# Query projection ahead of the third scores, value products behind them, and a front of its own, in an attention and adapter kernel on one core

## What is computed

```python
q = rope(rmsnorm(x @ Wq.T) * q_norm_w)      # 32 heads
k = rope(rmsnorm(x @ Wk.T) * k_norm_w)      # 8 heads
v = x @ Wv.T                                # 8 heads
k_all = concat(k_cache[block_table], k)     # 512 cached + 128 new keys per batch
v_all = concat(v_cache[block_table], v)
scores = q @ k_all.T / sqrt(128)            # cached keys beyond cache_seqlens are masked
x = x + softmax(scores) @ v_all @ Wo.T
```

## Time and profile before

| what | value |
| --- | --- |
| runs (median; lowest, highest) | 1185.21 us (1185.18, 1185.74) |
| the profiled execution's own time | 1183.14 us |
| its span in the profile | 1181.3 us |
| TensorE matmuls (PE) | busy 1146.3 us, 97% |
| VectorE (DVE) | busy 923.3 us, 78% |
| ScalarE (ACT) | busy 932.1 us, 79% |
| GpSimd (POOL) | busy 766.3 us, 65% |
| chain that ended last | PE 87%, DVE 5%, ACT 3%, issue 2% |
| TensorE idle for the first turned queries (L1115) | 9.1 us, once |
| TensorE idle at turned probabilities (L1042) | 6.6 us |
| HBM traffic | 82 GB/s over the span |

### The profile page before, as it was taken

One profiled execution on the slowest core, in us unless ns is written; L12 is line 12 of the kernel. 1 busy time (PEld: TensorE's weight loads), 2 busy tenths in 40 slices (PEclk: granted clock), 3 DMA queues, 4 the chain that ended last, 5 costly groups with the idle time before them and its releaser, 6 DMA issues.

```text
span 1181.3 us, 20774 instructions
## 1 busy us (share of the span) xinstructions
PE 1146.3 (97%) x6912; PEld 1024.1 (87%) x6912; DVE 923.3 (78%) x1880; ACT 932.1 (79%) x1830; POOL 766.3 (65%) x838
## 2 busy tenths in 40 slices
PE   4799999999999999999999999999999999999898
PEld 3688898998899898989988998989899889989787
DVE  6788888787778777887877787778878777877746
ACT  3787888888888888888888888888888888888741
POOL 5566666677676667676766766677667667666500
PEclk9899999999999999999999999999999999999999
DMA  6423412221232222122212222221232122111001
GB/s 240 127 79 97 148 53 89 95 88 54 94 95 70 72 94 95 51 91 94 88 55 95 94 66 77 94 95 50 93 94 83 58 93 92 59 67 55 19 1 72
DMA packets 53626, 98.11 MB, mean 83 GB/s; under 512 B 8592, under 2 KB 25872, under 8 KB 53264
## 3 DMA queue, kind: packets, MB, share of 16 engines
q1 hardware_dynamic: 41232, 63.21, 15.4%
q0 software_dynamic: 12288, 33.57, 9.6%
HBM read 90.45 MB, written 6.29 MB: 82 GB/s over the span
## 4 chain that ended last, share of the span: by engine, by line
PE 87%; DVE 5%; ACT 3%; issue 2%; DMA 1%; SPq 1%; POOL 0%; DVEq 0%; POOLq 0%
PE ps_s L1011 18%; PE ps_w L282 17%; PE ps_w L280 17%; PE ps_w L281 17%; PE ps_w L1042 9%; PE ps_w L1133 3%; PE ps_w L1115 2%; PE ps_s L993 2%; PE ps_w L1019 2%; ACT ps L527 2%; DVE pt_lo L664 1%; ACT ps L533 1%; DMA y<-wo 1%; DVE ps L727 1%; PE ps_w L1032 1%
## 5 line engine op out<-in xcount | busy, mean ns | idle before, releaser
L406 POOL DMA_INDIRECT kv_raw<-kv,rows x256 | 253.6, 991 | 93.8 <-issue 62.7
L527 ACT ACTIVATE ps<-ps,negmax 128x640 f32<-128x640 f32 x256 | 211.9, 828 | 97.9 <-DVE negmax L727 97.8
L664 DVE TENSOR_TENSOR pt_lo<-ps_w,pt_hi 128x512 fp32r<-128x512 f32 x322 | 209.9, 683 | 75.7 <-ACT pt_hi L538 74.4
L533 ACT ACTIVATE ps<-ps,recip 128x640 f32<-128x640 f32 x256 | 213.0, 832 | 67.4 <-DVE recip L734 67.4
L727 DVE CUSTOM_DVE_ANT_0 ps<-ps_s,mask 128x640 f32<-128x640 f32 x256 | 203.8, 814 | 1.1 <-PE ps_s L1011 1.1
L280 PE MATMUL ps_w<-w_hi,xt_hi 128*128 128x512 f32 (+1 forms) x512 | 188.9, 369 | 10.0 <-DVE w_lo L664 8.3
L282 PE MATMUL ps_w<-w_hi,xt_lo 128*128 128x512 f32 (+1 forms) x512 | 173.6, 339 | 0.0
L281 PE MATMUL ps_w<-w_lo,xt_hi 128*128 128x512 f32 (+1 forms) x512 | 173.1, 338 | 0.0
L427 POOL TENSOR_TENSOR rot<-u,cos 128x640 f32<-128x640 f32 x64 | 101.5, 1587 | 110.0 <-DVE u L783 110.0
L538 ACT ACTIVATE pt_hi<-ps_w 128x512 fp32r<-128x512 f32 x256 | 151.7, 593 | 17.8 <-PE ps_w L1042 15.0
L1042 PE MATMUL ps_w<-cst,ps 128*128 128x128 f32 x1024 | 154.1, 273 | 6.6 <-DVE pt_lo L664 5.9
(11 more groups left out here) (155 smaller groups left out, 2625.0 us busy)
## 6 DMA issues: line engine op xcount, KB each, us to landing
xt_hi<-xsplit SPq DMA_DIRECT2D x56, 256.0 KB, 3.2
xt_lo<-xsplit SPq DMA_DIRECT2D x56, 256.0 KB, 3.7
w_raw<-wqkv SPq DMA_DIRECT2D x56, 192.0 KB, 3.9
wo_raw<-wo SPq DMA_DIRECT2D x56, 128.0 KB, 4.2
kv_raw<-kv,rows POOLq DMA_INDIRECT x256, 3.9
xsplit<-xt_hi SPq DMA_DIRECT2D x8, 256.0 KB, 2.9
xsplit<-xt_lo SPq DMA_DIRECT2D x8, 256.0 KB, 4.2
y<-x SPq DMA_DIRECT2D x2, 1024.0 KB, 7.4
```

The lines of the kernel that those rows point to most:

```text
L406: pool.indirect_dma_start(kv_raw[:, g % 2, t, :], None, kv[:, :], bass.IndirectOffsetOnAxis(rows[:, g % B, t:t + 1], 0)).then_inc(s_kv[g % ...
L527: nc.scalar.activation(ps[:, h, :], ps[:, h, :], ACT.Exp, bias=negmax[:, s % 2, h:h + 1], scale=-1.0, accum_out=rowsum[:, s % 2, h:h + 1]) ...
L533: nc.scalar.activation(ps[:, h, :], ps[:, h, :], ACT.Copy, scale=recip[:, s % 2, h:h + 1]).then_inc(a_norm, 1)
L664: return nc.vector.tensor_tensor(out_ap, full, hi.bitcast(F32), ALU.subtract)
```

## The change

It has four parts. (1) In a step, TensorE computes the queries of g2 right behind scores 0 and 1, then scores 2, then the values of s - 1; ScalarE and VectorE follow with their reads (on VectorE o_lo now comes behind the sine product m). `UNITS` starts with Q instead of O ahead of T0. (2) Steps -2 and -1 are replaced by a front written out by hand on each engine: key and value weights are loaded and split first, g = 0 is multiplied by the plain norm weights, rotated on VectorE and scaled by the inverse norms afterwards, in five pieces on two engines; TensorE starts with WARM = 20 transposes. The angle is reduced in two parts instead of three. (3) The splits of the first output weights, the masks of batches 2 to 7, the split of x tile 3 and the bias rows move into steps 0, 1, 2 and 8. (4) The tables of the weight pieces change, with a second place in a step (`W_MID`, `WO_MID`); x tiles 2 and 3 are split into space of the second weight buffer. Natural x comes in eight loads instead of two.

The core of the diff, with "..." where lines are left out:

```diff
-TWO_PI_A = 6.28125
-TWO_PI_B = float(np.float32(int((TWO_PI - TWO_PI_A) * 2**20) / 2**20))
-TWO_PI_C = float(np.float32(TWO_PI - TWO_PI_A - TWO_PI_B))
+TWO_PI_A = round(TWO_PI * 2**12) / 2**12
+TWO_PI_B = float(np.float32(TWO_PI - TWO_PI_A))
...
-UNITS = ["O", "T0", "Q", "T1", "Y", "T2", "QT", "KTC", "KV", "KTN", "T3", "TN"]
+UNITS = ["Q", "O", "T0", "T1", "Y", "T2", "QT", "KTC", "KV", "KTN", "T3", "TN"]
...
-W_AT = {}
-for h in range(1, HK + 1):
-    for j in range(B):
-        W_AT.setdefault((0, 0, 1, 2, 2, 3, 4, 4)[j] if h == 1 else B * h - 11 + j, []).append((h - 1) * B + j)
-WO_AT = {s: [s] for s in range((HK - 1) * B + 2)}
+W_AT = {2: [2], 3: [4], 4: [6], 5: [7]}
+W_MID = {1: 0, 2: 1, 3: 3, 4: 5}
+for n in range(B, HK * B):
+    W_AT[n - 2] = [n]
+WO_AT = {3: [0], 4: [1], 5: [2], 6: [4], 7: [6], 8: [7]}
+WO_MID = {6: 3, 7: 5}
+for n in range(B, (HK - 1) * B + 2):
+    WO_AT[n + 1] = [n]
 RING = 3
+WARM = 20
...
+        def split_cols(g):
+            if 2 <= g < HB:
+                return w_hi[:, 1, (g + 2) * KC * S:(g + 3) * KC * S], w_lo[:, 1, (g + 2) * KC * S:(g + 3) * KC * S]
+            return xt_hi[:, g % 2, :], xt_lo[:, g % 2, :]
...
             def natural_x(half):
 
                 sp.wait_ge(d_xlo, (half + 1) * HB)
-                sp.dma_start(y[:, half * HB:(half + 1) * HB, :], x[half * HB:(half + 1) * HB].rearrange("b s h -> s b h")
-                             ).then_inc(s_y[half], 16)
+                for j in range(HB):
+                    sp.dma_start(y[:, half * HB + j, :], x[half * HB + j]).then_inc(s_y[j], 16)
...
-            for s in range(-2, G):
+            for s in range(G):
+                if s == 0:
+                    keep_x(2)
+                    keep_x(3)
+                    natural_x(0)
+                    sp.wait_ge(d_wolo, REP)
+                    x_transposed(2, 1, 0, 4)
+                if s + 1 in W_MID:
+                    w_load(W_MID[s + 1])
                 for n in W_AT.get(s + 1, ()):
                     w_load(n)
...
+                elif n == B - 3:
+                    act.wait_ge(pe_kv, HB)
+                    act.wait_ge(s_xkept[0], 64)
+                    act.wait_ge(s_xkept[1], 64)
...
```

ScalarE, in a step (the reads of queries and exponential 2 now ahead of o_hi):

```diff
+                if has(g2):
+                    queries(g2)
+                turn_x(s, "Q")
+                if has(s):
+                    if HB <= s + 3 < B:
+                        split_x(s + 3)
+                    exps(2)
+                    norm(2)
                 if has(s - 1):
                     wait(act, pe_o, s - 1)
...
                 if has(s):
                     probs(1)
+                    if s in W_MID:
+                        w_split(W_MID[s])
+                    if s in WO_MID:
+                        wo_split(WO_MID[s])
                     exps(3)
...
```

VectorE, in a step and in the front:

```diff
+                if s in (1, 2):
+                    masks(3 * s - 1, 3 * s + 1)
                 for n in W_AT.get(s - 1, ()):
                     w_split(n)
                 for n in WO_AT.get(s - 1, ()):
                     wo_split(n)
+                if has(s):
+                    rowmax(2)
+                if s == 0:
+                    split_x(3)
+                if has(g1):
+                    wait(dve, p_wr, g1 - 1)
+                    wait(dve, d_ss, g1)
+                    nc.vector.tensor_tensor(u[:].rearrange("p h d -> p (h d)"), raw[:, g1 % 2, 0:QW + D],
+                                            wr[:].rearrange("p h d -> p (h d)"), ALU.mult).then_inc(d_u, 1)
+                if has(s):
+                    over_sum(2)
+                if has(g1):
+                    times_sine(g1)
                 if has(s - 1):
                     wait(dve, a_o, s - 1)
                     low(o_lo[:], bank("O"), o_hi[:]).then_inc(d_olo, 1)
...
+                if HB <= s + 3 < B:
+                    split_x(s + 3)
+                if s == 0:
+                    first_wo_split(0)
+                    first_wo_split(1)
                 if has(s):
                     probs(2)
...
+                if s in W_MID:
+                    w_split(W_MID[s])
+                if s in WO_MID:
+                    wo_split(WO_MID[s])
+                if has(g1):
+                    new_keys(g1)
+                if s in (1, 2):
+                    masks(3 * s + 1, 3 * s + 2)
...
+                if s == B:
+                    biases()
...
+            first_kv_low(1)
+            less_turns(TWO_PI_A)
+            first_w_low(0)
+            less_turns(TWO_PI_B)
+            for k in range(1, KC):
+                first_w_low(k)
...
+            nc.vector.tensor_tensor(u[:].rearrange("p h d -> p (h d)"), raw[:, 0, 0:QW + D], nw[:].rearrange("p h d -> p (h d)"),
+                                    ALU.mult).then_inc(d_u, 1)
+            sums_of_squares(0)
+            dve.wait_ge(d_tab, 1)
+            times_sine(0)
+            dve.wait_ge(a_sincos, 2)
+            nc.vector.tensor_tensor(rot[:].rearrange("p h (t d) -> p (h t) d", t=2), u[:].rearrange("p h (t d) -> p (h t) d", t=2),
+                                    cos[:, 0, :].unsqueeze(1).to_broadcast([P, 2 * NH, HALF]), ALU.mult).then_inc(d_cos, 1)
...
+            for h in range(2, NH):
+                nc.vector.tensor_scalar(rot[:, h, :], rot[:, h, :], rstd[:, h:h + 1], None, ALU.mult).then_inc(d_scaled, 1)
...
+            masks(0, 2)
+            for s in range(G + 1):
                 step(s)
```

TensorE:

```diff
+            def project_queries(g):
+                if g < B:
+                    pe.wait_ge(d_xlo, g + 1)
+                else:
+                    pe.wait_ge(s_xback[g % 2], 32 * ((g - B) // 2 + 1))
+                    if g % B == 0:
+                        pe.wait_ge(d_wlo, SPLITS + g)
+                if g >= 2:
+                    wait_bank(pe, g - 2, "Q")
...
                     scores(1)
                 if s == G:
                     second_layer(0)
+                if has(g2):
+                    project_queries(g2)
+                turn_x(s, "Q")
+                if has(s):
+                    scores(2)
                 if has(s - 1):
...
+                if s == 0:
+                    project_keys_values(g2)
...
+            pe.wait_ge(s_cst, 16)
+            for _ in range(WARM):
+                nc.tensor.transpose(ps_s[:, 0, 0, 0:P], ident, ident)
+            pe.wait_ge(d_xlo, 1)
+            project_keys_values(0)
+            project_queries(0)
+            project_queries(1)
+            turn_cached_keys(0)
+            project_keys_values(1)
+            turn_queries(0)
+            turn_new_keys(0)
+            for s in range(G + 1):
                 step(s)
```

More of the change, by code:

```diff
@@ L876, in _ @@
+            dve.wait_ge(d_rot, 2)
+            wait(dve, p_rstd, 0)
+            for h in range(2, NH):
+                nc.vector.tensor_scalar(rot[:, h, :], rot[:, h, :], rstd[:, h:h + 1], None, ALU.mult).then_inc(d_scaled, 1)
+            cached_keys(0)
+            split_x(2)
+            turned_queries(0)
+            new_keys(0)
+            dve.wait_ge(s_kpos, 16)
+            masks(0, 2)
+            for s in range(G + 1):
                 step(s)
@@ new lines, in turn_new_keys, with project_keys_values, between @@
+            def turn_new_keys(g):
+                if g == 0:
+                    wait(pe, a_kv, 0)
+                else:
+                    wait_bank(pe, g - 1, "KTN")
+                nc.tensor.transpose(bank("KTN")[:, 0:S], rot[:, REP, :], ident).then_inc(pe_ktn, 1)
+            def project_keys_values(g, new_keys_of=None):
+                if g == 1:
+                    wait(pe, a_q, 0)
+                elif g >= 2:
+                    wait_bank(pe, g - 2, "KV")
+                def between(k):
+                    if g == 0:
+                        pe.wait_ge(d_wlo, k // 2 + 1)
+                    if new_keys_of is not None and k == KC - 1:
+                        turn_new_keys(new_keys_of)
+                wh, wl = head_weights(g // B)
+                three_passes(keys_values_bank(g)[:, 0:2 * D], [(xt_tile(0, g, k), xt_tile(1, g, k), wh[:, k, QW:WW], wl[:, k, QW:WW])
+                                                      for k in range(KC)], before=between).then_inc(pe_kv, 1)
@@ new lines, in turn_queries, with turn_cached_keys @@
+            def turn_queries(g):
+                if g == 0:
+                    pe.wait_ge(a_scaled, 2)
+                    pe.wait_ge(d_scaled, NH - 2)
+                    wait(pe, a_q, 1)
+                else:
+                    wait(pe, p_rot, g - 1, 2)
+                    wait_bank(pe, g - 1, "QT")
+                for h in range(REP):
+                    last = nc.tensor.transpose(bank("QT")[:, h * S:(h + 1) * S], rot[:, h, :], ident)
+                last.then_inc(pe_qt, 1)
+            def turn_cached_keys(g):
+                wait_kv(pe, g)
+                wait_bank(pe, g - 1, "KTC")
+                for t in range(CT):
+                    last = nc.tensor.transpose(bank("KTC")[:, t * P:(t + 1) * P], kv_raw[:, g % 2, t, 0:D], ident)
```

(1 more changed line is left out.)

415 lines of the change are left out of this document (202 added, 213 removed).

## The result

| what | before | changed |
| --- | --- | --- |
| runs, us (median; lowest, highest) | 1185.20 (1185.18, 1185.74) | 1224.12 (1222.40, 1225.85) |
| ratio to before, 95% interval | 1 | 1.0327 [1.0309, 1.0345] |
| profiled execution, span | 1183.14, 1181.3 | 1224.33, 1222.5 |
| mean granted clock (share of full speed) | 0.994 | 0.976 |

The change makes the kernel 38.9 us slower. The forecast was 1211 us with a range of 1197 to 1226; the time lies between it and the range's top, 5 us above rival 1 (seven falls of the clock, 1219).

The account below looks back on a forecast made before the run. TensorE's own stream was taken to bound the kernel, 17.10 us a step. Terms summed to +26.3 on the profiled 1183.14 (1209.4), 1211.5 at the runs' median, given as 1211; range 1197 to 1226.

Parts of the forecast that it names:

- rival 1: All seven stalls of TensorE drop its clock to half: 7.5 us more, 1219 us; chance 0.25.
- Part 1, front: Work ahead of the first scores: shorter chain to them, 11 us won (bounds 8 and 14), first scores near 23.
- step 0: VectorE's queue sets this step, with output weight splits and masks at its head: 1 us off, between 0 and 4.
- steps 1 to 5: Added work moves to where VectorE idles, some overruns delay row maxima: 3 us off, between 0 and 5.
- bias rows, o_lo chain, other effects in steps 6 to 61: Bias rows delay step 9's first row maximum, 1.5 us once; o_lo just in time, 0.03 a step, 1.5 us.
- falls of the clock: Stalls may drop TensorE's clock, 2.1 us each: none to seven falls, 0 to 15, half taken, 7.5 us on.
- tail: Steps 62 and 63: without queries the output product comes early, meets o_lo and turned x: 1 us on, -1 to 3.
- term (a): In the front: without output weights in between, the square of the queries starts earlier; 5.5 less 1, 4.5 us won.
- rival 2: VectorE's sine product loses the race to GpSimd's: output product 0.8 late in some 55 steps, 44 more, 1255; chance 0.10.
- Part 4: Queries wait for a head's last weight piece, split in the same step: 4.26 us, seven times, 29.8 on.
- Rival 3: The last weight piece is ready in time, so the stalls cost nothing: faster, 1174 us; chance 0.07.
- Rival 4: Stalls are there, but early steps don't gain as splits push the row maxima: 1216 us; 0.58 jointly with forecast.

Follow-up runs that it names:

- Experiment 3: Changed kernel with weight pieces split a step earlier and the old order of a step on all engines, new front kept; chip A: 1176.57 us, ratio 0.9931.
- 11: The same kernel as Experiment 3 (old order, early weight table, new front), timed again on chip C: 1175.44 us, ratio 0.9916.
- Experiments 1: Kernel before with only the weight table changed, each piece split one step later; chip A: 1184.23 us, ratio 0.9992.
- experiment 9: Changed kernel with weight pieces split a step earlier, the same program as experiment 2, on chip C: 1179.41 us, ratio 0.9947.
- Experiment 6: Changed kernel with 36 unused transposes ahead of each of the seven waits for the last weight piece; chip B: 1248.71 us, ratio 1.0539.
- experiment 5: Changed kernel with early weight table, VectorE's turned x split ahead of o_lo, bias rows halved over steps 8 and 9; chip A: 1213.35 us, ratio 1.0247.
- experiment 2: Changed kernel with weight pieces split a step earlier; chip A: 1218.92 us, ratio 1.0289.
- experiment 10: The kernel of experiment 9 with a memset of an unused tile on VectorE ahead of the sine product; chip C: 1178.36 us, ratio 0.9941.
- experiment 4: Changed kernel, unchanged, timed again on chip B: 1264.73 us, ratio 1.0673 to the kernel before.

## Why the prediction was right, and where it was off

In the terms of the sum, in spans (1181.3 to 1222.5, +41.2; the forecast's sum was +26.3):

| step of the prediction | forecast | measured |
| --- | --- | --- |
| Part 1, front | -11 | -9.7 |
| step 0 | -1 | +0.9 |
| steps 1 to 5 | -3 | -2.1 |
| bias rows, o_lo chain, other effects in steps 6 to 61 | +3 | -1.5 |
| seven stalls (queries 4.26 later; measured 4.24) | +29.8 | +29.7 |
| falls of the clock | +7.5 | +17.5 |
| tail | +1 | +6.4 |

The number fell into the range by luck in part: the same program took 1264.73 us on chip B, 39 above the range, by a delay that no term or rival has.

**Front.** Right in mechanism, 1.3 off, and all of it in term (a). Against 4.5 + 5.1 + 1.8 and 0.4 off for the rest, the trace gives 3.1 + 5.2 + 1.8 and 0.4 off: the square starts at 16.85 and not near 15.4, m at 18.36, the last sum ends at 20.91, the first scores start at 24.26. The square waits for the queries, which ScalarE reads only at 16.19. In the other profiles with this front the first scores lie between 23.2 and 26.3, so 1.3 is within what differs from run to run. Experiment 3 shows that this part is the gain.

**Steps 0 to 5.** The forecast took 1 us off step 0 where 0.9 came on. With the old order and the same front step 0 takes 17.32 (experiments 3 and 11) and with the new order 18.03 to 18.07 in all profiles but one, so 0.7 of it belongs to the new order; the rest may be the splits and masks at its head. What the fall of the clock at 36.83 costs in it isn't shown.

**The order in a step.** The hand timeline held to 0.02 us at every point of an ordinary step, and with it the claim that o_lo arrives just in time. The bias rows cost 1.0 in step 9 (18.07) instead of 1.5. The ordinary step is 0.05 below 17.10 rather than 0.03 above it; that is the negative entry (steps 6 to 61 took 1003.5 instead of 957.8 us, +45.7, less 29.7 and 17.5). What I didn't see is how much hangs on "just in time". I had noted 0.1 us of margin and put a chance on one way of losing it, the race. On two of the chips it was lost by another, a late signal of the scores, for 40 us. "m at 0.82" was right for ordinary steps only: in the seven long ones the race was lost, by rival 2's own condition (row maximum 2 started at 12.45 of step 30, against "later than about 6.4"), and cost nothing.

**The stalls.** Part 4 is right in place, number and length: the queries start 6.08 into the step against 6.10, 4.24 later than the 1.84 of an ordinary step, seven times. (TensorE's idle time is shown as 4.1, since the product before ends at 2.00.) Experiments 1 and 9 show that both parts of the change are needed for them.

**The clock.** This is the step that was mis-sized. "From none to seven falls, I take half" should have been seven (rival 1, chance 0.25, is what happened), and each cost 2.5 us instead of 2.1: 47.2 over the ordinary step, less 29.7, over seven. Experiment 6 gave 2.4 by itself. The Trainium skill's rule on idle gaps between bursts (TensorE: Matmul & The Clock Gate, "Why this matters for your kernels") was the better guide here, and the trace agrees: every one of the seven pauses of 4.1 us lowered the clock. I had weighed it against an idle of 2.4 us that did no harm, which said nothing about 4, and not even about 2.4: in step 0 of the changed kernel the clock fell behind an idle of 2.42, with another of 0.44 and four transposes just ahead of it, and in step 62 during one of 3.53.

**The tail.** The forecast's 1 covered "the turned x" without following it. `turn_x` moved with the queries on every engine; on VectorE it ended behind the split of probabilities 0, and by the renamed banks the output product waits for it. Steps 62 and 63 needed a hand timeline of their own, as the ordinary step had. In experiment 5, where that split stands ahead, step 62 and what follows it are 6.9 us shorter than in experiment 2.

Rival 3 (ready in time) is out by the rows above. Rival 4 (no gain in early steps) lies nearer than the forecast: steps 0 to 5 gained 1.2 us together, where 4 were forecast and rival 4 has none. Rival 2's price in an ordinary step stays unmeasured after experiment 10.

**What stays open** is why the signals of scores 0 and 1 come late on chips A and B. The profile shows when they rise, not why. They are there with both tables and both orders, and experiment 9's program has them on A and not on C, so neither table nor order alone makes them. But the order bears on their size: on chip A the old order has 40 of some 250, by 0.9 us at most (experiments 1 and 3), the new one 110, by up to 1.7 (experiments 2 and 5). What they have in common is the place, the first 4 us of a step, where the loads for the next steps run. The kernel before was timed on all three within 1 us but profiled once, so that it meets them on A and B and absorbs them is inferred from experiments 1 (40 late signals, and 1184.23 us) and 3.

## What to carry to other kernels

When a consumer moves forward in an engine's order, look up every producer's place in the step for the worst instance (here the head's last piece), not for the usual one; and do it for the last steps, where other work takes the banks. A stall of TensorE like these has to be priced with its fall of the clock, here 4.2 us for the wait and 2.5 for the clock each, and shorter idles shouldn't be counted free on the strength of one that was. A dependency that is met within 0.1 us can't be relied on: move its producer ahead of work that nobody waits for (o_hi ahead of a normalisation), and time the kernel on more than one chip before believing it.

## What the runs showed of the hardware that was not expected

- Completion signals of TensorE's score products reached VectorE 0.2 to 1.7 us after the product's modelled end, in 110 of 251 cases in experiment 2 (chip A), in 111 of 251 in experiment 4 (chip B) and in none of the four profiles on chip C. All of them were due in the first 2 us of a step. The same program took 1218.92 and 1179.41 us.
- Transposes raised and held TensorE's clock: behind 20 of them at 3.23 us a product at 8.29 took 0.28 instead of 0.42 us, and 36 in each stall saved 2.4 us a stall.
- The clock fell to half during waits of 4.1 and 3.53 us and once behind one of 2.42, while an empty stretch of 2.40 in the kernel before left it full.
- VectorE's sine product at 0.05 and 0.09 us behind GpSimd's still ran at full speed (0.76 us, GpSimd's 2.2), at 0.07 in another step it took 2.18 (GpSimd's 1.57), at 0.25 1.99. The recorded starts don't order the two to better than that.
